# Layer 0 of a two-layer graph network on one core, rewritten without hardware loops

## What is computed

```python
h = relu(layernorm(x))                                  # layer 0
A, B = adj @ h, adj @ (h @ W_gcnb) + b_gcnb
ga, gb = sigmoid([A, h] @ Wa.T + ba), sigmoid([A, h] @ Wb.T + bb)
hh = h @ W_sa
s = (hh @ a_sa[:256])[:, None] + (hh @ a_sa[256:])[None, :]
e = where(adj != 0, exp(-leaky_relu(s, 0.01)), 0)
xa = (e / (e.sum(1) + 1e-5)) @ hh
x = x + sigmoid(ga * xa + gb * B)
h = relu(layernorm(x))                                  # layer 1: two layers of
for W in W_stack:                                       # softmax attention
    Wh, Ws = split(h @ W)
    h = leaky_relu((softmax(Wh @ Ws.T) * adj) @ Wh + h, 0.01)
x = x + h
```

## Time and profile before

| | us |
|---|---|
| median of three runs | 1778.88 (1777.68 to 1782.95) |
| the profiled execution | 1779.5 |
| its span, first to last instruction | 1777.8 |

### The profile page before, as it was taken

How to read it: one execution, slowest core, us unless ns; L and a number is a source line. 1 busy time by engine, 2 the same in 40 slices (tenths; PEclk the granted TensorE clock), 3 DMA queues, 4 the chain that set the end, 5 groups by cost and what they waited for, 6 DMA issues and landing times.

```text
span 1777.8 us, 37615 instructions
## 1 busy us (share of the span) xinstructions
PE 1605.1 (90%) x12902; PEld 1566.8 (88%) x12902; DVE 1366.3 (77%) x2262; ACT 1064.0 (60%) x1980; POOL 1198.8 (67%) x1024
## 2 busy tenths in 40 slices
PE   3898888888888689999999999998999999999994
PEld 3898878887888589999999999997999999999984
DVE  6798888888888556777777777774778777777774
ACT  3766656666566746666656666663666666665663
POOL 1166665655665106888888888882888888888886
PEclk9999999999899899999999999999999999999999
DMA  4065555656655200001000100420011111111110
GB/s 136 16 117 112 102 106 113 122 105 127 112 115 111 72 1 13 32 32 40 33 32 32 44 32 32 128 90 8 27 32 32 38 33 40 42 33 32 33 39 18
DMA packets 76382, 107.38 MB, mean 60 GB/s; under 512 B 7393, under 2 KB 45280, under 8 KB 76000
## 3 DMA queue, kind: packets, MB, share of 16 engines
q1 hardware_dynamic: 48384, 91.25, 16.6%
q0 software_dynamic: 24336, 11.09, 8.0%
q10 hardware_dynamic: 3536, 3.41, 0.6%
HBM read 81.53 MB, written 24.18 MB: 59 GB/s over the span
## 4 chain that ended last, share of the span: by engine, by line
PE 51%; DVE 18%; issue 14%; POOL 11%; ACT 4%; DVEq 0%; POOLq 0%; DMA 0%; SPq 0%; ACTq 0%
PE PS L1156 25%; PE PS L1329 7%; PE PS L1332 7%; PE PS L1331 7%; DVE FR L892 5%; POOL FR L455 5%; POOL X L448 4%; DVE AF L888 4%; DVE AF L881 4%; POOL AF L430 2%; DVE AF L1025 1%; ACT FR L680 1%; DVE MV L802 1%; PE PS L1217 1%; PE PS L1218 1%
## 5 line engine op out<-in xcount | busy, mean ns | idle before, releaser
L455 POOL TENSOR_TENSOR FR<-AF,FR 128x512 fp32r<-128x512 f32 x338 | 448.7, 1328 | 162.5 <-ACT FR L680 161.2
L1156 PE MATMUL PS<-FR,RB 128*128 128x256 f32 x4056 | 544.2, 283 | 10.4 <-DVE RB L1077 5.4
L1156 PEld LDWEIGHTS PS<-FR,RB 128*128 128x128 f32 x4056 | 503.8, 189 | 18.9 <-ACT X L662 11.8
L448 POOL TENSOR_TENSOR X<-X,ROW 128x512 f32<-128x512 f32 x294 | 398.0, 1354 | 117.1 <-ACT ROW L690 117.1
L1329 PE MATMUL PS<-FR,RA 128*128 128x256 f32 x1352 | 389.3, 288 | 26.2 <-POOL FR L455 26.1
L1332 PE MATMUL PS<-FR,RA 128*128 128x256 f32 x1352 | 379.3, 281 | 0.0
L1331 PE MATMUL PS<-FR,RA 128*128 128x256 f32 x1352 | 378.8, 280 | 0.0
L430 POOL TENSOR_TENSOR AF<-ROW,SR 128x512 f32<-128x512 f32 x169 | 222.2, 1315 | 222.7 <-DVE FR L892 154.1
L1025 DVE TENSOR_TENSOR AF<-PS,A 128x512 f32<-128x512 f32 x338 | 231.2, 684 | 79.7 <-ACT PS L674 78.6
L1329 PEld LDWEIGHTS PS<-FR,RA 128*128 128x128 f32 x1352 | 254.3, 188 | 38.2 <-POOL FR L455 35.8
L1217 PE MATMUL PS<-RA,FR 128*128 128x258 f32 x676 | 202.2, 299 | 74.6 <-DVE FR L892 42.2
(11 more groups left out here) (145 smaller groups left out, 2711.3 us busy)
## 6 DMA issues: line engine op xcount, KB each, us to landing
ROW<-adjt SPq DMA_DIRECT2D x169, 256.0 KB, 3.0
A<-adj_scratch SPq DMA_DIRECT2D x26, 512.0 KB, 3.6
adj_scratch<-ROW POOLq DMA_DIRECT2D x169, 64.0 KB, 2.3
A<-adj_scratch SPq DMA_DIRECT2D x26, 320.0 KB, 2.9
xt_scratch<-ROW SPq DMA_DIRECT2D x12, 512.0 KB, 2.6
RB<-xt_scratch SPq DMA_DIRECT2D x12, 512.0 KB, 5.9
x_scratch<-X ACTq DMA_DIRECT2D x13, 256.0 KB, 2.2
ROW<-x_scratch SPq DMA_DIRECT2D x13, 256.0 KB, 4.0
```

The costliest lines, as they stand in the source:

```text
L448: nc.gpsimd.tensor_tensor(slot, slot, MB.unsqueeze(1).broadcast_to([P, 2, 256]), ALU.subtract)\
L455: nc.gpsimd.tensor_tensor(LO[g % 2], WA[g % 2], HI[g % 3].bitcast(F32), ALU.subtract)\
L1156: last = nc.tensor.matmul(out, stationary(a, k), moving(b, k), start=(k == 0 and i == 0), stop=(k == K - 1 and i == 2))
```

## The change

Layer 0 is rewritten with all pairs and units written out, as layer 1 was. Layer 1's steady part keeps its instructions; some of its buffers lie elsewhere.

- The addition and the leaky ReLU become two ACT operations of 256 columns (Prelu with the score column as bias). POOL's addition, DVE's leaky step and ACT's copy of adj are gone.
- The adj tile is loaded by POOL's queue with a cast to float32r, straight to a staging slot that DVE masks with and PE multiplies with. It is free once PE has done the unit and the byte store has landed. POOL's queue is now: store_bytes(n), load_unit(n + 6), and so on; every 13 units, behind the unit with k = 9, a small power for the layer normalisation.
- PE's accumulators alternate between banks 0 to 3 and 4 to 7 from pair to pair. ACT no longer copies the e banks; DVE reads them later.
- Units 0 to 10 are run between the projections (unit p - 2 behind pair p).
- x is loaded in other parts, tiles 0 and 1 first; statistics and scales are taken in five parts, most of them between projections; the square root and one reciprocal become a power on POOL and a correction step on DVE.
- Each pair's new x is normalised during the next pair's units. Layer 1's weight products and the transposes of x (all but the last pair's) run between the units of the last pair, and its first six projections before scores(0), not in steps 0 to 5.
- The order of DVE in unit step n is mask0(n + 2), low0(n + 1), then the post step of the pair before.

The diff, cut to its core:

```diff
-X_PARTS = [(0, 8), (8, 16), (16, 22), (22, T)]
+X_PARTS = [(0, 2), (2, 6), (6, 14), (14, T)]
+LN_PARTS = [(0, 2), (2, 6), (6, 10), (10, 18), (18, T)]
+LN_STATS = {0: (6, 10), 1: (10, 14), 2: (14, 18), 3: (18, 22), 4: (22, 26)}
+LN_CHAIN = {0: 2, 2: 3, 5: 4}
...
+def ah(n):
+    return n % 2 if n < UNITS else (0, 1, 8)[n % 3]
+def al(n):
+    return 2 + n % 2 if n < UNITS else (2, 3, 6)[n % 3]
...
-WH_AT = {v: (v + 1,) for v in range(6)}
-WH_AT |= {13: (7, 8), 14: (9, 10), 15: (11, 12)}
+WH_AT = {13: (6, 7, 8), 14: (9, 10), 15: (11, 12)}
...
+        def acc(pr):
+            return 4 * (pr % 2)
+        def turn(pr, i):
+            return 6 * pr + i + 1 if i else max(6 * pr - 5, 0)
+        def bank_of(pr, i):
+            return 4 + turn(pr, i) % 4
...
+            sp.dma_start(X[:, 0:2, :], xt[:, 0:2, :]).then_inc(x_in[0], 16)
+            sp.dma_start(WRAW0[:, :, 0:GX + D + 2], wx).then_inc(w_in, 16)
+            sp.dma_start(AROW, rows[:, 0:2 * D]).then_inc(w_in, 16)
+            for i, (t0, t1) in enumerate(X_PARTS[1:]):
+                sp.dma_start(X[:, t0:t1, :], xt[:, t0:t1, :]).then_inc(x_in[i + 1], 16)
...
-            def load_unit(pr, u, first):
-                b, n = before(STAGE, u), STAGE[:u].count(STAGE[u])
-                if not (first and n == 0):
-                    read = sp.to_reg(pr * UNITS + (LEAD + b + 1))
-                    stored = sp.to_reg(pr * (16 * stage_uses[STAGE[u]]) + 16 * n)
-                    sp.wait_ge(w_ready, 2)
-                    sp.wait_ge(adjr_done, read)
-                    sp.wait_ge(masked, read)
-                    sp.wait_ge(bytes_out[STAGE[u]], stored)
-                sp.dma_start(STG[:, STAGE[u], :],
-                             adjt[bass.ds(pr, 1), :, 2 * u:2 * u + 2, :].rearrange("o p j i -> p (o j i)"))\
-                    .then_inc(stage_full[STAGE[u]], 16)
...
-                    nc.gpsimd.tensor_tensor(
-                        AF[:, s, :].rearrange("p (j i) -> p j i", j=2),
-                        SLB[:, bass.ds(pr * 256, 256)].unsqueeze(1).broadcast_to([P, 2, 256]),
-                        SR[:, 2 * u:2 * u + 2].unsqueeze(2).broadcast_to([P, 2, 256]),
-                        ALU.add).then_inc(s_done, 1)
-                    landed = pool.to_reg(staged(pr, u))
-                    pool.wait_ge(ident, 1)
-                    pool.wait_ge(stage_full[STAGE[u]], landed)
-                    pool.wait_ge(ident, 1)
-                    pool.dma_start(adj8_d[bass.ds(pr, 1), :, 2 * u:2 * u + 2, :].rearrange("o p j i -> p (o j i)"),
-                                   STG[:, STAGE[u], :]).then_inc(bytes_out[STAGE[u]], 16)
...
+            def load_unit(n):
+                pr, u = n // UNITS, n % UNITS
+                if n >= NSTG:
+                    pool.wait_ge(mm_done, n - NSTG + 1)
+                    pool.wait_ge(bytes_out[n % NSTG], 16 * (n // NSTG))
+                pool.dma_start(STG[n % NSTG], adjt[pr, :, 2 * u:2 * u + 2, :].rearrange("p j i -> p (j i)"))\
+                    .then_inc(stage_full[n % NSTG], 16)
+            def store_bytes(n):
+                pr, u = n // UNITS, n % UNITS
+                pool.wait_ge(stage_full[n % NSTG], 16 * (n // NSTG + 1))
+                pool.dma_start(adj8_d[pr, :, 2 * u:2 * u + 2, :].rearrange("p j i -> p (j i)"),
+                               STG[n % NSTG].bitcast(F32)).then_inc(bytes_out[n % NSTG], 16)
+            def inverse_root(n, t0, t1):
+                pool.wait_ge(ln_in, n + 1)
+                nc.gpsimd.tensor_tensor(LNT[:, 1, t0:t1], LNT[:, 0, t0:t1], NHALF[:, 0:t1 - t0], ALU.pow)                  .then_inc(ln_pow, 1)
+            pool.wait_ge(half_set, 1)
+            inverse_root(0, *LN_PARTS[0])
+            inverse_root(1, *LN_PARTS[1])
+            for n in range(NSTG):
+                load_unit(n)
+            for n in range(2, len(LN_PARTS)):
+                inverse_root(n, *LN_PARTS[n])
+            for n in range(UN):
+                store_bytes(n)
+                if n + NSTG < UN:
+                    load_unit(n + NSTG)
+                pr, k = n // UNITS - 1, n % UNITS
+                if pr >= 0 and k == 9:
+                    inverse_root(len(LN_PARTS) + pr, 2 * pr, 2 * pr + 2)
+            inverse_root(len(LN_PARTS) + PAIRS - 1, T - 2, T)
...
+            def leaky0(n):
+                pr, u = n // UNITS, n % UNITS
+                act.wait_ge(slb_done, pr + 1)
+                act.wait_ge(sr_done, 2 * u + 2)
+                if n >= NWORK:
+                    act.wait_ge(lo_done, n - NWORK + 1)
+                for jj in range(2):
+                    last = nc.scalar.activation(AF[:, n % NWORK, jj * 256:(jj + 1) * 256],
+                                                SLB[:, pr * 256:(pr + 1) * 256], ACT.Prelu,
+                                                bias=SR[:, 2 * u + jj, :], alpha=SLOPE)
+                last.then_inc(lr_done, 1)
+            def exp0(n):
+                act.wait_ge(lr_done, n + 1)
+                nc.scalar.activation(AF[:, n % NWORK, :], AF[:, n % NWORK, :], ACT.Exp, scale=-1.0)\
+                  .then_inc(e_done, 1)
+            def high0(n):
+                act.wait_ge(masked, n + 1)
+                if units_before(ah, n):
+                    act.wait_ge(mm_done, units_before(ah, n))
+                nc.scalar.activation(FR[:, ah(n), :], AF[:, n % NWORK, :], ACT.Copy).then_inc(hi_done, 1)
...
+            for n in range(UNITS - 2, UN):
+                pr, k = n // UNITS - 1, n % UNITS
+                if n + 3 < UN:
+                    leaky0(n + 3)
+                if n + 2 < UN:
+                    exp0(n + 2)
+                if n + 1 < UN:
+                    high0(n + 1)
+                if pr >= 0:
+                    if k == 3:
+                        post_gates(pr)
+                    if k == 4:
+                        post_gated(pr)
+                    if k == 6:
+                        post_sigmoid(pr)
+                    if k == 7:
+                        post_sigmoid2(pr)
+                    if k == 9:
+                        post_store(pr)
+                    if k == 11:
+                        normalise1(pr)
...
+            def scales(n, t0, t1, stats):
+                v, r, t, rstd, nmr = (LNT[:, i, t0:t1] for i in (0, 1, 2, 4, 5))
+                h = LNT[:, 3, t0:t1]
+                dve.wait_ge(stat_d, stats)
+                for i in range(t0, t1):
+                    last = nc.vector.bn_aggr(MV[:, i, :], BN0[:, i, :])
+                last.then_inc(aggr_d, 1)
+                dve.wait_ge(aggr_d, n + 1)
+                nc.vector.tensor_scalar(v, MV[:, t0:t1, 1], EPS_LN, None, ALU.add).then_inc(ln_in, 1)
...
+                dve.wait_ge(ln_pow, n + 1)
+                nc.vector.tensor_tensor(t, r, r, ALU.mult).then_inc(ln_step, 1)
...
+            dve.wait_ge(x_in[0], 16)
+            statistics(0, 2)
+            scales(0, 0, 2, 1)
...
+            def mask0(n):
+                s = AF[:, n % NWORK, :]
+                dve.wait_ge(e_done, n + 1)
+                dve.wait_ge(stage_full[n % NSTG], 16 * (n // NSTG + 1))
+                nc.vector.tensor_tensor(s, s, STG[n % NSTG].bitcast(F32), ALU.mult).then_inc(masked, 1)
+            def low0(n):
+                dve.wait_ge(hi_done, n + 1)
+                if units_before(al, n):
+                    dve.wait_ge(mm_done, units_before(al, n))
+                nc.vector.tensor_tensor(FR[:, al(n), :], AF[:, n % NWORK, :], FR[:, ah(n), :].bitcast(F32),
+                                        ALU.subtract).then_inc(lo_done, 1)
...
+            def post_norm(pr):
+                dve.wait_ge(x1_ready, pr + 1)
+                statistics(2 * pr, 2 * pr + 2)
+                scales(len(LN_PARTS) + pr, 2 * pr, 2 * pr + 2, 2 + len(LN_STATS) + pr + 1)
...
+            for n in range(UNITS - 2, UN):
+                pr, k = n // UNITS - 1, n % UNITS
+                if n + 2 < UN:
+                    mask0(n + 2)
+                if n + 1 < UN:
+                    low0(n + 1)
+                if pr >= 0:
+                    if k == 2:
+                        post_bias(pr)
+                    if k == 4:
+                        post_weights(pr)
+                    if k == 5:
+                        post_mix(pr)
+                    if k == 8:
+                        post_x1(pr)
+                    if k == 9:
+                        post_norm(pr)
...
+            post_bias(PAIRS - 1)
+            xt_low(10)
+            post_weights(PAIRS - 1)
+            wh_low(0)
+            post_mix(PAIRS - 1)
+            xt_low(11)
+            wh_low(1)
+            post_x1(PAIRS - 1)
             q_low(0)
-            wh_low(0)
-            xt_low(2)
+            post_norm(PAIRS - 1)
+            wh_low(2)
+            wh_low(3)
+            wh_low(4)
+            wh_low(5)
...
+            def unit0(n):
+                pr, u = n // UNITS, n % UNITS
+                if u == 0 and pr == 1:
+                    pe.wait_ge(glo_done, T)
```

(105 more changed lines are left out.)

690 lines of the change are left out of this document (269 added, 421 removed).

## The result

The changed kernel takes **1980.9 us** (median of four runs, 1979.3 to 1981.7) against 1778.3 for the kernel before: 1.112 times its time, 95% interval 1.111 to 1.114. I had forecast 1764.2 and a range of 1715 to 1812, so it is slower where I had said faster, and outside the range. Up to scores(0) the kernel grew by 214 us (845.5 against 631.4); layer 1's steady part kept its time.

A forecast was written before the change was run, and what follows sets the result against it. DVE, with POOL's addition, set the old unit; afterwards POOL's loads every 3.2 us would. Sum: 106 + 486.4 + 8.7 + 2 + 14 + 14.6 + 20.6 + 1110.2 + 1.7 = 1764.2 us, range 1715 to 1812.

The forecast's parts named there:

- P: POOL's queue in layer 0's units: one round of load issue, store landing and queueing, taken as 3.2 us; break-even at 3.3.
- my own formula: Whole kernel: the forecast time as 1277.8 + 152 P, in us.
- queueing behind the load: POOL's queue: what a store loses behind the load ahead of it, up to 0.33 us of each round P.
- the far end: POOL's queue: the store moves nothing before the load has landed, so P is 4.6 and the time 1977 us.
- rival C: POOL's queue: store waits longer behind the casting load, or that load costs POOL over 0.6; slower from P = 3.3; 25%.
- tail to scores(0): From the units' end to layer 1's scores(0): 14.6 us instead of 28.9, set by DVE's post_norm chain, two groups and an eviction.
- ramp: Layer 1 from scores(0) to its steady part: 12 steps at 1.6 us plus 1.4 for a projection, 20.6 instead of 36.2.
- Start: Preamble and projections: first product near 19 us instead of 29.7, projections ending at 106 with 11 units done.
- Engines in the units: Layer 0's units: PE needs 2.4 us, ScalarE 2.0 to 2.5, DVE's mask and low 2 x 0.60.
- Rival D: ScalarE in the units: table changes between Prelu and Exp, twice a unit at 1.28 us, about 2070 us; 3%.
- Meetings: Once per pair, DVE's post_norm at k = 9 waits about 10 us for POOL's power; charged 1.2 us x 12 = 14.
- Rival A: Layer 0's units: POOL's round is hidden and PE sets the unit at 2.4 us, 1655 us in all; 7%.

The follow-up runs named there:

- e6: The changed kernel with an unused power of four columns (1.02 us) on GpSimd between each load and the store that follows it: 2000.0 us, a single execution.
- e8: The kernel of e5 with the byte stores issued two places ahead instead of one: 1651.9 us, 0.927 of the kernel before.
- e4_power_early: The changed kernel with GpSimd's power for a pair's norm moved from behind the load of k = 9 to between store and load of k = 7: 1992.4 us.
- e1: The changed kernel with each byte store issued one place earlier on GpSimd, ahead of the staging load that precedes it now: 1689.2 us, 0.950 of the kernel before.
- e5: The kernel of e1 with the power for the norm put between the store and the load of k = 8: 1666.9 us, 0.935 of the kernel before.

## Why the prediction was wrong

**The step that failed is P, POOL's round.** The mechanism was named rightly ("Every unit POOL therefore sits out one whole store"), its size was not: 3.2 predicted, 4.48 in a plain round. Two terms of one sum were wrong:

- *The time from the landing to the next issue was put at nothing.* I added the load's issue and the store's "from issue to landing", as if the next load started when the store has landed. It starts 0.53 us later. The trace of before had such a wait: POOL's store at 151.31 waited for a load that SP issued at 147.94 (the first of four in a row) and that landed after 2.7, at 150.6, so POOL needed 0.7 us there.

```profile
147.94 2.89 SPq L319 DMA_DIRECT2D ROW<-adjt  x4
...
151.31 0.57 POOL L439 DMA_DIRECT2D adj_scratch<-ROW  x1 [4.21 <-DMA ROW<-adjt]
```

  152 x 0.53 = 81 us. With this alone P would have been 3.73, and by my own formula the time 1277.8 + 152 x 3.73 = 1845: slower.
- *The queueing behind the load was mis-sized.* I allowed 0 to 0.33, by subtracting the 0.60 between the issues from 0.93 of packets. The store lost 1.1 (3.42 against 2.3). A head start of 1.6 us for the load removes it (e6), one of 0.53 doesn't. So a transfer's packets do not run right behind its issue: the load of 399.93 has landed at about 403.2, 3.3 us after the start of its issue, and the store of 400.46 at about 403.9. 152 x (1.12 - 0.3) = 125 us.

Against these, 0.53 lie between the starts of the load and the store where I had 0.60 (-11). What exceeds 4.48 in the mean, 0.145 a round, is 22 us, about 15 of them in the 28 rounds with a fetch of instructions (5.00 against 4.48). Together 703.0, the distance from load 16 to load 168, against 486.4.

The price was within my reach: the far end, "if the store moved nothing before the load has landed", was P = 4.6 and 1977 us, and stands in the text. I gave everything beyond P = 3.51 only 7%, though no row showed two transfers in a row on this queue. The value should have been taken from the ends, and rival C should have had most of the chance: it needed 0.1 us more than I had taken, and had one unmeasured term on its side.

**The sum against the trace:**

| stage | predicted | measured |
|---|---|---|
| until load 16 is issued | 106 | 113.7 |
| loads 17 to 168 | 486.4 | 703.0 |
| meetings, added transposes | 16 | in the row above |
| last load to the last matmul of the units | 8.7 | 13.0 |
| tail to scores(0) | 14.6 | 15.8 |
| ramp | 20.6 | 23.7 |
| steady layer 1 and around the span | 1111.9 | 1112.1 |
| total | 1764.2 | 1981.3 (the profiled execution) |

- *Start: right.* The first product is at 18.67 (I said 19; 29.73 before) and the projections end at 107.4 (106). Load 16 left 6.3 us after they ended (113.7), since the slow chain of loads had begun with load 6 at 68.89 and not after them.
- *Engines in the units: right.* The mask takes 0.69 us in each of the 169 units and never the 1.52 of the earlier trace rows (where it ends 0.55 us after POOL's addition, not with it, as I had read). A Prelu takes 494 ns, by the earlier trace rows 495. With the loads out of the way PE's 2.40 us set the unit (e8), as in the earlier trace rows.
- *Rival D, tables: fell.* The whole kernel loads one table, where the kernel before loaded six:

```profile
0.74 1.28 ACT L463 ACT_TABLE_LOAD   x1 [0.74 <-PEq L1423]
```

- *Meetings: found, but mispriced.* They look as predicted, DVE idle for 13.68 us behind the power, PE for 14.19, and then a lower clock: PE was busy for 1.16 of 14 us, and in the 13 us behind that the granted clock is 0.72 of 2.4 GHz in the mean, so the lower level, 1.2 GHz, held for a part of them. Order of time, and then the two stretches:

```profile
410.33 0.16 DVE L758 TENSOR_TENSOR LNT<-LNT 128x2 f32<-128x2 f32 x1 [13.68 <-POOL LNT L415]
412.35 0.58 PE L1182 MATMUL PS<-RA,FR 128*128 128x258 f32 x1 [14.19 <-DVE FR L822]
```
```profile
397.00:411.00 14.00, 1.16 (x10) 0.95 (x8) 0.56 (x4) 0.00 (x0) 3.93 (x7) 0.65 0.46 78
411.00:424.00 13.00, 11.65 (x74) 11.65 (x75) 8.01 (x14) 10.10 (x22) 2.73 (x6) 0.72 0.40 66
```

  I charged 14 us for them; e4_power_early shows that taking them away brings nothing while the loads are this slow. The power takes 0.72 us, not 0.4; the one on eight columns takes 1.64, above the 1.31 that I had called a bound.
- *Slips in the working:* 3.2 is more than the 3.05 us that a unit took before, not "hardly less", and the 61 us won around the units come to 63 (14.3 in the gap, 15.6 in the ramp, 33 in start and projections). The total had both right.
- *Rival A, 1655:* the mechanism I gave 7% is what one changed line of order produces (e1), and its price was good: 1651.9 in e8.

**What stays open:** why a round with a fetch of instructions is 1.1 us longer in e4_power_early and 0.5 in the changed kernel. In both its packets are as many. PE runs evenly in the one and in bursts in the other, so the fetches may fall at other places of a round; no run told these apart. What POOL does in the 0.53 us between a landing and its next issue isn't shown by the profile. A staging load without the cast on this queue wasn't tried, so no run tells whether the cast has a part in the 3.4.

## What to carry to other kernels

Where an engine issues a transfer and its next instruction waits for that same transfer, the whole latency stands in the loop: the issues ahead of it, the landing, and the time until the next issue starts (0.53 us here), and the landing grows by what lies ahead in the queue. Look for the youngest transfer that each wait names, count how many rounds cover it, and move the issue rather than the wait: one place earlier was worth 292 us here, a second one a further 15. When a round on the critical path contains a term that no row shows, take its far end as seriously as its near one, above all if the break-even lies next to the value taken.

## What the runs showed of the hardware

- Two transfers in a row on GpSimd's queue: a 64 KB store issued 0.54 us behind a 256 KB casting load lands 3.4 us after the start of its issue, behind a 128 KB one after 2.5, with nothing right ahead of it after 2.3.
- GpSimd's issue of a transfer starts 0.53 us after the landing that it waited for. This is no part of the landing.
- Landings of 4.3 us and DMA engines busy for 89% did not slow units of 2.4 us once the stores were issued two rounds ahead (e8). One round ahead, with landings of 3.8 us (e5), nearly hid them: 15 us remained.
- Instructions are fetched while the kernel runs, over the same DMA engines. Between 90 and 600 us the looped kernel before had 2 packets on the instruction queue q8, the changed one 18. A round with such a packet took 0.5 to 1.1 us longer. This price of writing out the loops wasn't in my sum.
